# Issuing all four mask operations of a head's two wide steps at the end of the previous head, in a fused attention and mixture-of-experts block on one Trainium2 core

## The reference

```python
for n in range(K_NODES):
    qr = q * cos[pos[..., n]] + rotate_half(q) * sin[pos[..., n]]
    kr = k * cos[pos[..., n]] + rotate_half(k) * sin[pos[..., n]]
    scores = einsum('bhid,bhjd->bhij', qr, kr) * SCALE
    scores = where(causal & member[..., n][:, :, None, :], scores, NEG)
    outs.append(einsum('bhij,bhjd->bhid', softmax(scores), v))
y = (tk_w[..., None] * gathered_two_nodes(outs)).sum(axis=3)
```

## Time and profile before

| | |
|---|---|
| median of 3 runs | 932.78 us (931.88 to 933.57) |
| the profiled execution | 932.19 us, its span 930.5 us |
| busy PE / DVE / ACT / POOL | 823.0 / 825.6 / 730.5 / 605.5 us |
| masks (L1111) | 256 operations, 100.0 us |
| TensorE clock granted | 0.978 of full speed |

### The profile page before, as it was taken

How to read it: one execution, slowest core, us unless ns; L and a number is a source line. 1 busy time by engine, 2 the same in 40 slices (tenths; PEclk the granted TensorE clock), 3 DMA queues, 4 the chain that set the end, 5 groups by cost and what they waited for, 6 DMA issues and landing times.

```text
span 930.5 us, 21666 instructions
## 1 busy us (share of the span) xinstructions
PE 823.0 (88%) x6544; PEld 578.3 (62%) x6544; DVE 825.6 (89%) x2124; ACT 730.5 (79%) x1999; POOL 605.5 (65%) x951
## 2 busy tenths in 40 slices
PE   4468989999999999999999999999999999899893
PEld 4455656666666666666566666666666666575793
DVE  6879989998999899989998999889988998787795
ACT  6357898888888888888888878887888887865572
POOL 4566668776866686668666766676556666127393
PEclk9779999999999999999999999999999999999997
DMA  9111222221222122212221222122111111423553
GB/s 208 40 24 39 44 41 48 45 44 32 54 42 45 32 50 44 44 39 47 44 45 38 48 45 44 38 48 39 22 18 23 26 26 18 129 69 92 145 166 114
DMA packets 106641, 51.13 MB, mean 55 GB/s; under 512 B 60672, under 2 KB 105664, under 8 KB 106528
## 3 DMA queue, kind: packets, MB, share of 16 engines
q1 hardware_dynamic: 105312, 47.24, 23.6%
q0 software_dynamic: 1216, 2.51, 0.8%
HBM read 36.91 MB, written 12.43 MB: 53 GB/s over the span
## 4 chain that ended last, share of the span: by engine, by line
PE 51%; DVE 25%; issue 10%; ACT 8%; POOL 3%; DMA 2%; SPq 1%; DVEq 0%; ACTq 0%; POOLq 0%
PE psum L1537 18%; PE psum L1560 8%; PE psum L1394 7%; PE psum L1549 6%; DVE pcs L1087 5%; ACT probs L768 4%; DVE accs L1137 3%; POOL R L533 3%; PE psum L1522 3%; PE psum L1585 3%; DVE negmax L1117 2%; DVE psum L1126 2%; DVE outside L1111 2%; PE psum L1540 2%; ACT QK L745 1%
## 5 line engine op out<-in xcount | busy, mean ns | idle before, releaser
L1537 PE MATMUL psum<-QK 128*128 128x128 f32 (+3 forms) x1024 | 370.6, 460 | 2.0 <-DMA wrow<-words 0.8
L768 ACT ACTIVATE probs<-psum,negmax 128x128 f32<-128x128 f32 (+3 forms) x512 | 267.0, 530 | 72.8 <-DVE negmax L1126 56.2
L533 POOL TENSOR_TENSOR R<-pcs 128x512 f32<-128x512 f32 x128 | 176.3, 1398 | 53.9 <-DVE pcs L1087 53.9
L1537 PEld LDWEIGHTS psum<-QK 128*128 128x128 f32 x1024 | 155.8, 192 | 48.7 <-issue 41.9
L1126 DVE CUSTOM_DVE_ANT_0 psum<-psum,outside 128x384 f32<-128x384 f32 (+1 forms) x256 | 154.9, 637 | 25.7 <-PE psum L1540 25.6
L559 POOL TENSOR_TENSOR coef<-rden,wslot 128x2 f32<-128x2 f32 x256 | 52.9, 207 | 180.3 <-DVE rden L1132 180.3
L1137 DVE SCALAR_TENSOR_TENSOR accs<-probs,coef,accs 128x128 f32<-128x128 f32 (+3 forms) x256 | 162.0, 633 | 2.0 <-ACT accs L777 2.0
L777 ACT ACTIVATE accs<-probs,coef 128x128 f32<-128x128 f32 (+3 forms) x256 | 148.7, 581 | 17.1 <-POOL coef L559 17.1
L1087 DVE TENSOR_TENSOR pcs<-psum,arena 128x512 f32<-128x512 f32 x256 | 161.7, 672 | 0.0
L1549 PE MATMUL psum<-ident,accs 128*128 128x128 f32 x640 | 116.7, 281 | 41.6 <-ACT QK L745 28.9
L745 ACT ACTIVATE QK<-psum 128x384 f32<-128x384 f32 x235 | 116.8, 497 | 2.4 <-PE psum L1524 2.3
(11 more groups left out here) (271 smaller groups left out, 1511.9 us busy)
## 6 DMA issues: line engine op xcount, KB each, us to landing
wrow<-words SPq DMA_DIRECT2D x64, 96.0 KB
weight_halves<-whl SPq DMA_DIRECT2D x48, 128.0 KB, 2.2
arena<-weight_halves SPq DMA_DIRECT2D x22, 256.0 KB, 3.1
wrow<-words SPq DMA_DIRECT2D x64, 86.0 KB
arena<-weight_halves SPq DMA_DIRECT2D x7, 512.0 KB, 6.9
wrow<-words SPq DMA_DIRECT2D x64, 42.0 KB
wst<-in_L_ffn_w_up_dram SPq DMA_DIRECT2D x14, 128.0 KB, 2.4
wst<-in_L_ffn_w_gate_dram SPq DMA_DIRECT2D x14, 128.0 KB, 2.4
```

The source lines that it names most:

```text
L533: pool.tensor_tensor(R[u][:, :, :, 0:3:2, half * HALF:(half + 1) * HALF].rearrange("p t e j f -> p (t e) j f"), halves(pc, half), halves(p ...
L768: act.activation((expB if e else expA)[:, k % (4 if e else 3), 0:w], area, ACT.Exp, scale=1.0 if k % TB < 2 else -1.0, bias=negmax[k % 4][ ...
L1537: pe.matmul(o, QK[:, u, e, rows], QK[:, u, 2, 0:w], start=True, stop=False)
```

## The change

The masks of steps 2 and 3 are no longer issued in front of a `row_max` of their own head. All four operations for the next head's steps 2 and 3 stand behind `inverse_sums` at the end of step 3; those of head 0 stand at the end of its step 0. A wait is added, that the row extremes that last read the two `outside` buffers are through; DVE makes them itself.

```diff
                 dve.wait_ge(S["codes_done"], 2)
+                if n:
+                    dve.wait_ge(S["negmax_done"], 2 * (k - TB) + 2)
                 dve.wait_ge(S[f"mm_in{n % RING}"], 64 * (n // RING + 1))
...
-                if k < STEPS and s == 0:
-                    place_outside(k + 2)
-                elif k < STEPS and s == TB - 1:
-                    place_outside(k)
                 if k < STEPS:
                     row_max(k)
...
                 if 1 <= k <= STEPS:
                     inverse_sums(k - 1)
+                if k == 0:
+                    place_outside(2)
+                    place_outside(3)
+                elif s == TB - 1 and n + 1 < NH:
+                    place_outside(k + 3)
+                    place_outside(k + 4)
```

## The result

The change made the kernel slower by about 3 us: 935.53 us median of 13 runs (932.99 to 938.62) against 932.25 (929.56 to 933.57) of the kernel before in 13 runs, a ratio of 1.0037 with a 95% interval of 1.0024 to 1.0050. The profiled execution took 933.92 us, its span 932.2. The prediction was 933.0 us (926 to 940); it had put no change at 0.35, slower at 0.34 and faster at 0.31, so the measured time lies within its range, on the side where it had one chance in three. Between 63 and 800 us of the span the granted clock is 1.00 in both traces, so the clock has no part in what happens in the loop.

The account below looks back on a forecast made before the run. PE and DVE were taken to bound the kernel by turns. The profiled 932.19 us + 3.2 (plain pairs) - 3.0 (angle pairs) gave 932.4; with the median 0.6 above that execution, 933.0 us, range 926 to 940.

Parts of the forecast that it names:

- Nothing is saved, the waits are free, DMAs don't move: Whole loop: 256 masks before and after, 465 and 395 ns each; added waits cost nothing; SP's queue runs as before.
- Even heads start 0.1 to 0.15 us behind PE: Step 0 of even heads: most of the moved masks' 0.77 us falls into DVE's 0.61 us wait for PE's scores.
- Plain pairs: Even heads n % 8 = 6 and late pairs without angles: relief lost to POOL, odd reduction late; +0.40 us each, +3.2 for eight.
- The pairs of 6 and 14: Plain pairs that already had the collision of DVE's multiply-add with POOL's L538, so left out of the +3.2 us.
- Angle pairs: Even heads n % 8 = 0 or 2: earlier masks bring ACT's copy and PE forward; -0.25 us each, -3.0 for twelve.
- The term for PE's lead: Angle pairs: of the 0.77 us PE gains, some 0.4 are left at the odd head's values, its transposes waiting for L552.
- Sine pairs: Even heads n % 8 = 4: as many masks as before, the even head's 0.1 us swallowed by a 1.10 us wait; 0.
- The sum: Whole kernel: 933.0 us, +0.2 against the median of 932.78 before.
- the rival without effect: Masks sink in waits on both sides, odd heads' reductions not late; 932.8 us, chance 0.10.
- the faster one: Even step 3: the multiply-add slips in ahead of POOL's L538 or L541, so relief is kept; 925.6 us, chance 0.24.
- The slower one: Odd heads: their delay reaches PE in full, 7.0 us in plain and 1.8 in angle pairs; 941.6 us, chance 0.26.

Follow-up runs that it names:

- e3: The kernel before with only the added wait on the row extremes put in front of each pair of masks; 932.50 us, ratio 1.0000.
- e6: The kernel before with even heads' step 2 masks before the previous odd head's step 3 extremes, their step 3 masks before their own first reduction; 920.03 us, ratio 0.9868.
- e1: The changed kernel with only even heads' step 3 masks moved early, odd heads' as in the kernel before; 922.19 us, ratio 0.9890 to the kernel before.
- e2: The changed kernel with only odd heads' step 3 masks moved early, even heads' as in the kernel before; 946.26 us, ratio 1.0147 to the kernel before.
- e7: e1 with POOL's coefficients of step 3 made before the rotation's L538 and L541; 938.93 us, ratio 1.0059 to the kernel before.
- e4: The changed kernel with its four masks directly behind step 3's row extremes, before the 128-column multiply-add; 945.81 us, ratio 1.0145 to the kernel before.
- e5: The changed kernel with POOL's coefficients of step 3 made before the rotation's L538 and L541; 939.49 us, ratio 1.0072 to the kernel before.
- e8: The kernel before without the step 3 masks of heads 1 to 63, their extremes using head 0's masks; 918.07 us, ratio 0.9844.

## Why the prediction was right or wrong

- **Nothing is saved, the waits are free, DMAs don't move**: right. Masks take 470 and 396 ns, e3 measures the added waits at 0 (give or take 1 us), and no mask operation waits for words any more.
- **Even heads start 0.1 to 0.15 us behind PE**: right in kind, 0.08 measured. DVE's waits there are gone but for head 0's, and the reductions start 0.18 or 0.19 us behind PE's last matmul, where it was 0.10 or 0.11. e6, which takes one pair away from this place, has 0.10 or 0.11 again, and plain and sine pairs 0.07 and 0.06 us shorter than e1.
- **Plain pairs, +0.40 us each**: right in mechanism, +0.34 measured. L1139 of 128 columns takes 1.02 us behind L538, the odd reduction comes at 10.22 (said: about 10.3), the pair at 21.84 (said: near 21.9). The pair of head 6 in the trace of before was the right measure for it, since it had the same collision. The way to PE is the one named: L552 ends at 431.51 and PE's transposes start 0.10 behind it, where they followed PE's scores without a pause before. The values begin 15.01 us behind the even head's first reduction instead of 14.75, and the rest is the next even head's 0.08.
- **The pairs of 6 and 14, no change**: wrong by 0.15 us each. They had the collision already and lost it, as DVE now comes before L538 (L1139 at 141.86, L538 at 142.46; 0.35 instead of 1.16 us).
- **Angle pairs, -0.25 us each, the step that failed.** PE's wait fell as far as it could (1.44 to 0.66) and L1139 took 0.71 us against POOL's L541, as worked out. But of PE's 0.77 us I had left 0.4 at the values, with L552 as what holds PE. It held nothing here: L552 ends at 477.74 and PE's transposes start at 478.23. They wait for ACT's copy, ACT's copies stand behind its exponentials, and these for the odd head's late reductions (0.22 and 0.28 us of waiting at 474.43 and 476.68). I had followed DVE to PE by way of POOL and not by way of ACT. The values begin at 479.00 instead of 479.15, with the even head's start 0.07 earlier too: 0.08 left of 0.77. The ten pairs from 16 on came out at -0.01, those of 8 and 10 at +0.10 and +0.17, so the twelve lie 3.2 us above the forecast. The term for PE's lead was the wrong one: 0.4 was to be left at the values.
- **Sine pairs, 0**: measured +0.08; six pairs, 0.5 us. It comes behind the odd head's first reduction, which lies at 13.90 in both traces. The even head's lateness is the likely source, since e6 takes 0.06 away, but no run moves it alone. e2 shows how little cover there is: the whole 0.77 goes through.
- **The sum**: +0.2 was said against the median of before, +3.3 measured. The angle pairs are nearly all of the difference; smaller misses partly cancel (sine pairs +0.5, plain pairs -0.5, those of 6 and 14 -0.3, and pairs 0 and 2, which the forecast took as unchanged, +0.51 and -0.78). That the time fell into the range says little for the mechanism, since the range held the rival without effect too; the pair lengths are the test, and one of the two main ones failed.
- **The rivals**: the faster one (relief not lost to POOL) is refuted by the 1.02 and 0.71 us. The slower one (the odd head's delay reaches PE in full) holds for sine pairs if odd masks alone are moved (e2), in plain pairs for four tenths (0.28 of 0.74). In angle pairs it was nearer than the forecast: it had PE's lead all lost, and 0.08 was left. The one without effect is refuted by the odd heads' reductions, 0.73 late in plain pairs.

What the change does is thus a sum of two halves of opposite sign: -11 us from the even heads (e1) and +13 from the odd ones (e2). The sum of the halves is +2.4, and both together gave +3.3 by the medians and +2.7 in the trace. That these are so close is chance, for the halves do interact. In plain pairs they add up (0.06 + 0.28 against 0.34). In angle pairs -0.72 + 0.33 would be -0.39, and both together are -0.01, since the odd head's masks undo the lead that the even head's step 3 gave PE. In sine pairs -0.28 + 0.77 would be +0.49 and is +0.08, in those of 6 and 14 -0.15 + 0.61 would be +0.46 and is -0.15.

What the signs go by is where DVE waits for PE in the kernel before. In front of even heads it waits 0.46 to 0.62 us, so a pair of masks is nearly free there, and in an even step 3 of an angle pair it is on the path. In front of odd heads DVE doesn't wait, and in an odd step 3 it waits 1.3 to 1.4 us in plain and sine pairs.

What stays open: why e7 loses as much as 17 us against e1. Its collisions and DVE's new wait for PE are seen, the 17 us were not divided among them.

## What to carry to other kernels

Before moving work along an in-order engine, list for each place the wait behind it, separately for each kind of iteration: the same move was worth -11 us in even heads and +13 in odd ones, and both together show +3. The price of two moves is not the sum of their prices either: in angle pairs the second undid the first. A relief is only worth what the next operation can use; here the next operation of DVE ran into one of POOL, and a change of order that removes one such collision can make another in every iteration (e4, e5). Leaving the suspected work out (e8) tells in one run about how much a rearrangement of it can give.

## What the runs showed of the hardware that I had not expected

Two engines' operations meet far more sharply than their durations suggest. A DVE multiply-add with two inputs in SBUF that starts 0.01 us behind a POOL operation of 0.62 us takes 0.89 us instead of 0.47 (e4). The later it starts, the less it pays: behind an L538 of 1.04 or 1.05 us the 128-column one takes 1.16 us when it starts 0.04 behind the earlier trace rows, 1.02 at 0.17 and 0.42 at 0.78. In all three cases it ends 1.19 or 1.20 us behind L538's start.

Which of the two pays goes by who starts first. In the kernel before, the 384-column L1137 starts 0.05 us ahead of L552 in head 31 and takes 0.61 us, and L552 takes 1.15 instead of 0.72. In head 35 it starts 0.04 behind L552 and takes 1.10. DVE in both heads, then POOL in head 31:

```profile
430.28 0.61 DVE L1137 SCALAR_TENSOR_TENSOR accs<-probs,coef,accs 128x384 f32<-128x384 f32 x1
...
476.56 1.10 DVE L1137 SCALAR_TENSOR_TENSOR accs<-probs,coef,accs 128x384 f32<-128x384 f32 x1
```

```profile
430.33 1.15 POOL L552 TENSOR_TENSOR ktoks<-R,kwork 128x256 f32<-128x256 f32 x1
```

The masks, a DVE operation with one 16-bit input, show nothing of this. In e4 four of them lie over an L538 and an L541 and take 1.51 us together, where four take 1.48 or 1.49 elsewhere, and their means are 465 to 472 and 395 to 404 ns in every run, so they serve as a spacer.

By the Trainium skill, "SBUF — State Buffer", section "SBUF: two separate sides", the pair of ports is held for a whole instruction by whoever starts first. The traces agree that the order of two starts a few hundredths of a microsecond apart decides; the wait is some 0.2 us shorter than what is left of the other operation in the profile (1.16 us at 0.04 behind, not 1.01 + 0.34 = 1.35). And e4 and e5 each paid the price in places where nothing had been moved.
